# Empty rows made by two engines and stored between the halves of x, in the first stage of a four-layer kernel

## The reference, cut to what matters

```python
x = x + 0.5 * _L0_ffn_ref(_layernorm(x, axis=-1), L0_ffn_wg, L0_ffn_W, L0_ffn_b)

def _L0_ffn_ref(x, wg, W, b):
    ...
    logits = xt @ wg
    probs = jax.nn.softmax(logits, axis=-1)
    idx = jnp.argmax(probs, axis=-1)
    mask = jax.nn.one_hot(idx, Ee, dtype=xt.dtype)
    locations = jnp.cumsum(mask, axis=0) - mask
    mask = mask * (locations < C).astype(xt.dtype)
    ...
```

## Time and profile before

| what | value |
|---|---|
| median of three runs | 1423.43 us |
| the profiled execution: its own time | 1418.19 us |
| the profiled execution: span from first to last instruction | 1417.0 us |
| busy: TensorE, VectorE, ScalarE, GpSimd | 78%, 67%, 58%, 23% of the span |

### The profile page before, as it was taken

The page is one execution under the profiler, slowest core; times in us unless marked ns, Lnnn a source line. Parts: engine busy times, 40 slices in busy tenths (PEclk is TensorE's granted clock), DMA queues, the critical chain, the costliest instruction groups (busy, mean ns, idle before and its releaser), DMA issues. The chain is left out here.

```text
span 1417.0 us, 30244 instructions
## 1 busy us (share of the span) xinstructions
PE 1107.5 (78%) x12280; PEld 905.5 (64%) x12280; DVE 943.1 (67%) x1619; ACT 827.6 (58%) x964; POOL 326.0 (23%) x409
## 2 busy tenths in 40 slices
PE   6273789888999899989889996563649965984797
PEld 3163665578888887548888884253318963642797
DVE  5113646789999985679999997313845645773365
ACT  7211444689999943388999995522623325753332
POOL 4755001000000000100000000756362430237244
PEclk9677799999999999999999998877669987997799
DMA  9955200302122100011121212283333333003243
GB/s 253 330 177 172 67 1 0 72 35 88 62 91 88 65 2 1 4 60 62 75 78 65 87 62 90 99 275 128 130 125 99 120 121 93 1 14 133 85 123 99
DMA packets 84468, 132.17 MB, mean 93 GB/s; under 512 B 14662, under 2 KB 71238, under 8 KB 79942
## 3 DMA queue, kind: packets, MB, share of 16 engines
q1 hardware_dynamic: 65984, 89.47, 20.0%
q0 software_dynamic: 13056, 35.87, 7.1%
q10 hardware_dynamic: 5292, 4.90, 1.1%
HBM read 82.38 MB, written 47.83 MB: 92 GB/s over the span
## 5 line engine op out<-in xcount | busy, mean ns | idle before, releaser
L1406 ACT ACTIVATE b_signs<-b_q_everywhere,normed 128x2048 bf16<-128x2048 f32 x224 | 429.2, 1991 | 24.5 <-PE banks L1293 23.3
L1293 PE MATMUL banks<-b_value_parts,b_signs 128*128 128x102 bf16 x8192 | 392.7, 208 | 40.5 <-DVE b_signs L1581 38.0
L1293 PEld LDWEIGHTS banks<-b_value_parts,b_signs 128*128 128x128 bf16 x8192 | 375.8, 97 | 60.2 <-DVE b_signs L1581 50.0
L1581 DVE TENSOR_SCALAR b_signs<-b_q_everywhere,normed 128x2048 bf16<-128x2048 f32 x288 | 350.8, 1278 | 8.3 <-PE banks L1293 8.3
L685 POOL DMA_INDIRECT moe_slots<-normed,slot_of_token x128 | 124.7, 975 | 39.1 <-issue 34.1
L1633 POOL MEMSET b_value_parts<- 128x256 bf16 x2 | 2.7, 1329 | 450.4 <-PE banks L1166 450.4
L439 PE MATMUL banks<-identity,normed 128*128 128x128 f32 x256 | 48.6, 322 | 54.7 <-ACT normed L374 54.6
L347 DVE BATCH_NORM_STATS2 ln_stats<-residual 128x6 f32<-128x256 f32 x192 | 71.3, 417 | 17.9 <-SPq L1827 10.5
L450 PE MATMUL banks<-normed_T,wg 128*8 128x256 f32 x256 | 73.0, 412 | 1.8 <-ACT normed_T L548 1.8
L439 PEld LDWEIGHTS banks<-identity,normed 128*128 128x128 f32 x256 | 31.6, 160 | 65.6 <-ACT normed L374 49.5
L374 ACT ACTIVATE normed<-residual,ln_shift,ln_rstd 128x256 f32<-128x256 f32 x128 | 68.1, 587 | 3.7 <-DVE ln_shift L369 3.7
(11 more groups left out here) (283 smaller groups left out, 2301.0 us busy)
## 6 DMA issues: line engine op xcount, KB each, us to landing
b_q_everywhere<-q_rows SPq DMA_DIRECT2D x32, 1024.0 KB, 4.7
normed<-expert_rows SPq DMA_DIRECT2D x6, 1024.0 KB, 10.2
d_rows<-moe_slots SPq DMA_DIRECT2D x40, 129.5 KB, 2.2
f_rows<-moe_slots SPq DMA_DIRECT2D x40, 129.5 KB, 2.2
moe_slots<-a_empty SPq DMA_DIRECT2D x8, 518.0 KB, 9.1
a_rows<-moe_slots SPq DMA_DIRECT2D x16, 259.0 KB, 3.0
c_rows<-moe_slots SPq DMA_DIRECT2D x16, 259.0 KB, 4.0
expert_rows<-a_empty SPq DMA_DIRECT2D x1, 4096.0 KB, 25.7
```

The lines of the kernel that those rows point to most:

```text
L1293: ins = nc.tensor.matmul(banks[qt // QPB][:, qt % QPB * VP:(qt % QPB + 1) * VP], t.SG[:, (hh * TB + kt) % RING, qt * P:(qt + 1) * P], t.VO ...
L1406: nc.scalar.activation(t.SG[:, g % RING, :], t.QB[:, hh % 2, :], ACT.Sign, bias=t.NKT[:, kt, hh % H:hh % H + 1]).then_inc(s.sign_a, 1)
L1581: nc.vector.tensor_scalar(t.SG[:, g % RING, :], t.QB[:, hh % 2, :], t.KTM[:, kt, hh % H:hh % H + 1], 2.0, ALU.is_gt, ALU.mult).then_inc(s. ...
```

## The change

- The part of `EMPTY` that holds zeros is written in halves: tiles 0-15 by VectorE, as its very first instruction (semaphore `empty_front`), tiles 16-31 by GpSimd. GpSimd makes the row numbers of all 32 tiles first (`empty_made` 1), then its half (`empty_made` 2). Most of its other constants come after that.
- SyncE issues the eight stores of empty rows after `x_in2` and ahead of `x_in3` and `x_in4`, the loads of tiles 16-23 and 24-31.
- VectorE places the first group of tokens ahead of the statistics of group 3 (tiles 16-19), not behind them.
- ScalarE takes a square root of a constant first, so that the table of that function is loaded at the start. TensorE and ScalarE no longer wait for all constants but for the identity and for eps; TensorE waits for all of them at its first count.

The diff, cut to its core:

```diff
@@ act_route
     if r == 0:
-        nc.scalar.wait_ge(s.consts, 1)
+
+        nc.scalar.wait_ge(s.eps_made, 1)
+        nc.scalar.activation(k.WARM[:, :], k.EPS[:, 0:1], ACT.Sqrt)
@@ dve_route
-        dve_statistics(k, stage, n0 + 3, *groups[3])
-        if r == 0:
+        if r:
+            dve_statistics(k, stage, n0 + 3, *groups[3])
+        else:
             nc.vector.wait_ge(s.consts, 1)
             nc.vector.wait_ge(s.gates_in, 48)
         dve_place(k, r, 0)
+        if r == 0:
+            dve_statistics(k, stage, n0 + 3, *groups[3])
         dve_scale(k, n0 + 3, *groups[3])
@@ sp_program
-    for sem, (lo, hi) in zip((s.x_in1, s.x_in2, s.x_in3, s.x_in4), CUTS[1:]):
+    for sem, (lo, hi) in zip((s.x_in1, s.x_in2), CUTS[1:3]):
+        nc.sync.dma_start(k.X[:, lo:hi, :], tiles_of(a["x"])[:, lo:hi, :]).then_inc(sem, 16)
+
+    nc.sync.wait_ge(s.empty_front, 1)
+    for e in range(E):
+        if e in (0, E // 2):
+            nc.sync.wait_ge(s.empty_made, 1 if e == 0 else 2)
+        nc.sync.dma_start(tiles_of(k.by_slot[e]), k.top0[0].EMPTY[:, e * CAP // P:(e + 1) * CAP // P, :]).then_inc(s.emptied, 16)
+    for sem, (lo, hi) in zip((s.x_in3, s.x_in4), CUTS[3:]):
         nc.sync.dma_start(k.X[:, lo:hi, :], tiles_of(a["x"])[:, lo:hi, :]).then_inc(sem, 16)
     for n, name in enumerate(("b1", "b2")):
         nc.sync.dma_start(k.BIAS[:, n, :], a[name].rearrange("o (p c) -> p (o c)", p=P)).then_inc(s.biases_in, 16)
-    nc.sync.wait_ge(s.empty_made, 1)
-    for e in range(E):
-        nc.sync.dma_start(tiles_of(k.by_slot[e]), k.top0[0].EMPTY[:, e * CAP // P:(e + 1) * CAP // P, :]).then_inc(s.emptied, 16)
@@ dve_program
+    nc.vector.memset(k.top0[0].EMPTY[:, 0:NT // 2, 0:D], 0.0).then_inc(s.empty_front, 1)
@@ pool_program
+    EMPTY = k.top0[0].EMPTY
+    nc.gpsimd.memset(k.EPS[:, 0:1], LN_EPS)
+    nc.gpsimd.memset(k.EPS[:, 1:2], STD_EPS).then_inc(s.eps_made, 1)
     nc.gpsimd.memset(k.IDENT[:, :], 0.0)
+    k.ps.step(nc.gpsimd.memset(EMPTY[:, :, D:RW], 0.0))
+    io(EMPTY[:, :, D:D + 1].bitcast(I32)[:, :, 0], [[P, NT]], T, 1).then_inc(s.empty_made, 1)
+    nc.gpsimd.affine_select(out=k.IDENT[:, :], ...).then_inc(s.ident_made, 1)
+    nc.gpsimd.memset(EMPTY[:, NT // 2:NT, 0:D], 0.0).then_inc(s.empty_made, 1)
...
-    k.ps.step(nc.gpsimd.memset(EMPTY[:, :, :], 0.0))
-    io(EMPTY[:, :, D:D + 1].bitcast(I32)[:, :, 0], [[P, NT]], T, 1).then_inc(s.empty_made, 1)
```

More of the change, by code:

```diff
@@ L121 @@
     "xn turned xtr logit lt lgt chosen counted pos slot scattered tables pads_from padded gaps exps gate "
-    "numbers_made empty_made emptied slots_empty w0_in xs_in0 xs_in1 xs_in2 xs_in3 xs_in4 xs_turned xs_row xst expert ys "
+    "eps_made ident_made numbers_made empty_front empty_made emptied slots_empty w0_in xs_in0 xs_in1 xs_in2 xs_in3 xs_in4 xs_turned xs_row xst expert ys "
     "back0 back1 back2 y0_zeroed spares_stored y_in0 y_in1 y_in2 y_in3 y_in4 "
@@ L185, in plan @@
     k.EPS = m.take("eps", [P, 2])
+    k.WARM = m.take("square_root_tried", [P, 1])
     k.NUMBER = m.take("empty_slots_rows", [P, NT, RW - D], I32)
@@ L386, in pe_route @@
     if r == 0:
-        nc.tensor.wait_ge(s.consts, 1)
+        nc.tensor.wait_ge(s.ident_made, 1)
         nc.tensor.wait_ge(s.gates_in, 48)
@@ L473, in pe_count @@
     before = k.bank[5][:, 0:E * (GROUP + 1)].rearrange("p (e t) -> p e t", e=E)
+    if r == 0 and g == 0:
+        nc.tensor.wait_ge(s.consts, 1)
     nc.tensor.wait_ge(s.chosen, r * NG + g + 1)
@@ L1893, in pool_program @@
                                                   allow_small_or_imprecise_dtypes=True)
+    EMPTY = k.top0[0].EMPTY
+    nc.gpsimd.memset(k.EPS[:, 0:1], LN_EPS)
+    nc.gpsimd.memset(k.EPS[:, 1:2], STD_EPS).then_inc(s.eps_made, 1)
     nc.gpsimd.memset(k.IDENT[:, :], 0.0)
+    k.ps.step(nc.gpsimd.memset(EMPTY[:, :, D:RW], 0.0))
+    io(EMPTY[:, :, D:D + 1].bitcast(I32)[:, :, 0], [[P, NT]], T, 1).then_inc(s.empty_made, 1)
+    nc.gpsimd.affine_select(out=k.IDENT[:, :], in_=k.IDENT[:, :], compare_op=ALU.not_equal, fill=1.0, base=0,
+                            pattern=[[-1, P]], channel_multiplier=1).then_inc(s.ident_made, 1)
+    nc.gpsimd.memset(EMPTY[:, NT // 2:NT, 0:D], 0.0).then_inc(s.empty_made, 1)
     nc.gpsimd.memset(k.UTRI[:, :], 1.0)
@@ L1899, in pool_program @@
     nc.gpsimd.memset(k.LAYERF[:, :, :], 1.0)
-    nc.gpsimd.memset(k.EPS[:, 0:1], LN_EPS)
-    nc.gpsimd.memset(k.EPS[:, 1:2], STD_EPS)
     nc.gpsimd.memset(k.PAD[:, :], 0.0)
     k.ps.step(nc.gpsimd.memset(k.CHOSEN[:, :, :], 0.0))
-    nc.gpsimd.affine_select(out=k.IDENT[:, :], in_=k.IDENT[:, :], compare_op=ALU.not_equal, fill=1.0, base=0,
-                            pattern=[[-1, P]], channel_multiplier=1)
     nc.gpsimd.affine_select(out=k.UTRI[:, :], in_=k.UTRI[:, :], compare_op=ALU.is_ge, fill=0.0, base=-1,
@@ L1916, in pool_program @@
     nc.gpsimd.tensor_copy(k.ROWS3B[:, :], k.LAYERF[:, 0, :])
+    nc.gpsimd.wait_ge(s.ident_made, 1)
     nc.gpsimd.tensor_scalar(k.MINUSI[:, :], k.IDENT[:, :], -1.0, None, ALU.mult)
@@ L1926, in pool_program @@
     io(k.NUMBER[:, :, 0], [[P, NT]], T, 1).then_inc(s.numbers_made, 1)
-    EMPTY = k.top0[0].EMPTY
-    k.ps.step(nc.gpsimd.memset(EMPTY[:, :, :], 0.0))
-    io(EMPTY[:, :, D:D + 1].bitcast(I32)[:, :, 0], [[P, NT]], T, 1).then_inc(s.empty_made, 1)
     pool_route(k, 0)
```

## The result

In one set of paired runs the kernel after takes 1425.08 us (median of 20, 1422.05 to 1429.64) and the kernel before 1421.91 (median of 20, 1419.21 to 1426.24). The ratio is 1.0022, 95% interval 1.0013 to 1.0031: the change costs 3.2 us, 1.9 to 4.4. The profiled execution took 1425.84 us with a span of 1424.6.

A forecast was written before the change was run, and what follows sets the result against it. The landing of the empty rows, set by DMA transfer time, was taken to bound the scatters; landing 5.8 us earlier but holding the second group gave +1.9 us, 1423.43 to 1425.3, range 1418.5 to 1430.5.

The forecast's parts named there:

- What bounds the stage: Up to SyncE's first read at 77.72 us: the later of the empty rows' landing and GpSimd finding groups ready.
- Halves, table load, lighter waits: Empty rows made in halves, early square-root table, fewer waits at the start: each forecast worth 0.
- the two bounds: VectorE's memset of its half: 3.5 us if as fast as GpSimd, 5.6 us from a statistics pass.
- The stores: Empty rows behind the third load of x: landing at 26.6 instead of 32.4, 5.8 us earlier.
- second rival: Half way: fourth load at 28.5 or a clock costing nothing, ninth scatter 42 to 44, 1421.5 to 1423.4; chance 0.2.
- The fourth load: x's load for tiles 16-23, queued behind the stores: forecast to land at 30.0 while sharing DMAs with scatters.
- its own sign: Stated test of failure: the prediction is wrong if the fourth load lands more than 3 us from 30.
- The hold of the second group: ScalarE's square root of group 3 waits until 31.8, 9.5 us later, holding second-group copies and logits queued behind it.
- The way to the slots: Square root of group 3 to the second group's slots: 10.7 us plus 2.4 for TensorE's low clock.
- The sum: End of the scatters: +1.9 us, 0 for the rest; profiled execution 1420.1, median 1425.3.
- third rival: TensorE's clock stays low through routing: third and fourth groups late, scatters end 8 us later, 1431.5; chance 0.1.

The follow-up runs named there:

- second_group_free: Kernel after with TensorE, ScalarE and VectorE finishing pairs 4 to 7 and the second placement before touching tiles 16 to 19; 1424.72 us, ratio to before 0.9996.
- stores_late: Kernel after with x's later half put back ahead of the stores in SyncE's queue, all else kept; 1425.0 us, ratio to before 0.9992.
- same_again: Kernel after, unchanged, profiled a second time on another chip; 1428.17 us in one execution.
- loads_wait: Kernel after with SyncE issuing the fourth and fifth load of x only once all eight stores have landed; 1430.29 us, ratio to before 1.0028.
- before_again: Kernel before, unaltered, profiled a second time; 1421.88 us.

## Why the prediction was right, and where it was off

**What bounds the stage.** Right. The later of two things sets it, the landing of the empty rows and the groups being ready, and second_group_free moves the end by the second alone.

**Halves, table load, lighter waits: nothing.** Right, shown by stores_late. VectorE's half took 3.47 us, at the lower of the two bounds (3.5 to 5.6), where the chosen middle came to 4.5. That it ended at 5.21, as if the forecast of 5.3 had been right, is luck: it began at 1.74 and not near 0.8. One cycle per element, as the Trainium skill has it ("VectorE: DVE Perf Modes", section "Zero memsets can be issued as uint32 (trn2)"), would have made it an estimated 4.3 us; the trace doesn't agree.

**The stores.** This is the step that failed: "The empty rows follow the third load: 11.3 + 15.3 = 26.6". They landed at 32.1 and, in same_again, 31.4. Of the 5.5 us, 0.8 are the third load, which landed at 12.1 in after. From there 15.3 us were taken over from before, where nothing lay behind the stores on their queue. loads_wait has that case after the change, and takes 16.2 (12.1 to 28.3). With the loads behind them they took 20.0, so 3.8 us of the miss are the queued loads. The 0.9 that is left is within what the stores vary by: before_again takes 16.4 for them (17.0 to 33.4) where before took 15.3. The 15.3 us were a fair price for the stores alone and not for stores with loads behind them. The second rival's idea that x could be moved in the stores' tail was borne out, but gained nothing: 0.98 MB of x was in before the stores' last packet, and yet the fourth load landed no sooner and the stores later.

**The fourth load.** Predicted 30.0, measured 34.75 and 34.04. That is outside the 3 us that the prediction set as its own limit, so by its own sign it was wrong here. The miss follows from the step above: the load landed some 2.6 us behind the stores, where 3.4 were forecast.

**The hold of the second group.** Right in every link. The square root came 1.72 us behind the load (1.8 forecast), ScalarE and TensorE stopped there, the next square root added nothing, and VectorE's slots released GpSimd. second_group_free shows that this order is the cause.

**The way to the slots.** Predicted 13.1, measured 12.54. The clock costs 1.7 us and not 2.4. TensorE was at 0.50 from the resumption at 37 to about 42, as the earlier trace rows had it; it was two pairs' worth, a little cheaper. The 1.88 us that the prediction took for half clock stand at 11.97, where the windows of before give 1.00 and not half; the reading holds all the same, since after has 1.87 at 37.30 with 0.50.

**The sum.** The ninth scatter was forecast at 45.9 and came at 49.68, 3.8 later, of which 4.75 are the load, -0.56 the way, -0.33 the step from the slots to the scatter (0.67 for 1.0) and -0.08 the step from the load to the square root. The loss in the stage is 5.7 us against before and, over both pairs of profiles, 4.9 (mean of 79.44 and 78.86, less that of 73.73 and 74.80). The third and fourth groups stayed hidden, so the third rival didn't occur, and all later stages kept the difference: at 868 us it is 4.7 (means of 873.27, 871.89 and of 867.96, 867.88).

**What is left open.** Medians differ by 3.2 us (1.9 to 4.4) where the profiles of the stage say 4.7 to 4.9. From the weights load of the third layer to the end, profiles of the same kernel differ by 3.7 us, 549.0 and 552.7 in the two of before and 551.3 and 555.0 in the two of after. The stage's loss and the medians could differ by that alone; it isn't shown. The forecast's 1.9 us is at the lower end of what the medians allow and less than half of what the stage lost, and only the lower median of before brought the time back to 1425.

## What to carry to other kernels

Moving a transfer ahead moves the wait to whatever it pushes back: follow that one through every engine that meets it in its written order, for work whose data is there may stand behind a wait that isn't its own. A stream's duration holds for the queue it was read in; put something behind or beside it and the price is open on both sides. If the later half must be late, reorder the engines so that only its own group waits for it, or give it another queue.

## What the runs showed of the hardware

- Loads of x queued behind stores on one queue made the stores land 3.1 to 4.0 us later (copies behind them at 32.20, 31.54 and 32.41 against 28.41; 31.29 against 28.09 on another chip). It hit the last tenth of the stores' packets, among which 0.98 MB of x was moved in after. Between 20 and 26 us the DMA share stayed at 1.07 or more while the rate fell to 162 to 222 GB/s.
- With the same loads on another queue the stores landed as late (32.5), but all of x had landed by 30.6 instead of 37.5; at 20 to 22 us 376 GB/s were moved. Why the rates differ is open: no run here varied the size or number of the stores.
- A memset of 128x4096 f32 by VectorE took 3.47 us, 0.85 ns per element, the same as GpSimd's 3.51 at the same time.
- TensorE's clock in after was 0.50 at 36 to 38 us, after a pause of 12.5 us, and 0.94 again at 42 to 44; the price was 1.7 us. Turns that ended 6.7 us before the work didn't keep it, turns that ran up to it did.
- One of three chips ran all the kernels some 2% slower.
